# The thirteen looped rounds of a layer written out one behind the other in a six-layer transformer kernel

## The reference

```python
for i in range(DEPTH):                    # 6 layers
    x = attn_layer(shift_tokens(x), Wqkv[i], q_scale[i], k_scale[i], Wo[i]) + x
    x = ffn_layer(shift_tokens(x), ln_g[i], ln_b[i], W1[i], b1[i], W2[i], b2[i]) + x
```

## Time and profile before

| | us |
|---|---|
| median of three runs (lowest, highest) | 3637.79 (3636.72, 3644.33) |
| the profiled execution | 3636.09 |
| its span from first to last instruction | 3634.3 |
| PE busy in the span | 3397.6 (93%) |
| DVE busy | 3109.7 |
| ACT busy | 2520.1 |
| POOL busy | 1849.6 |

### The profile page before, as it was taken

The page is one execution under the profiler, slowest core; times in us unless marked ns, Lnnn a source line. Parts: engine busy times, 40 slices in busy tenths (PEclk is TensorE's granted clock), DMA queues, the critical chain, the costliest instruction groups (busy, mean ns, idle before and its releaser), DMA issues.

```text
span 3634.3 us, 161649 instructions
## 1 busy us (share of the span) xinstructions
PE 3397.6 (93%) x63524; PEld 2729.1 (75%) x63524; DVE 3109.7 (86%) x6016; ACT 2520.1 (69%) x4543; POOL 1849.6 (51%) x1604
## 2 busy tenths in 40 slices
PE   5857999999999999999999999999999999999997
PEld 2325888878788877788887788887788887788885
DVE  8987888888788888788888788888788888888884
ACT  2015777777777777777777677777677777777774
POOL 1434655554555555456555465555455564555561
PEclk9988999999999999999999999999999999999998
DMA  2002423323333323333233432332423332323333
GB/s 83 12 26 54 103 60 79 75 57 82 87 77 77 71 62 77 89 79 74 57 79 70 96 75 60 76 78 56 107 63 73 79 73 61 77 66 70 79 75 79
DMA packets 186363, 261.00 MB, mean 72 GB/s; under 512 B 31670, under 2 KB 89908, under 8 KB 185396
## 3 DMA queue, kind: packets, MB, share of 16 engines
q1 hardware_dynamic: 186164, 258.24, 31.6%
HBM read 22.30 MB, written 4.19 MB: 7 GB/s over the span
## 4 chain that ended last, share of the span: by engine, by line
PE 83%; issue 8%; DVE 5%; ACT 1%; POOL 1%; SPq 1%; DMA 0%; DVEq 0%; ACTq 0%; POOLq 0%
PE bank L667 10%; PE bank L654 9%; PE bank L719 9%; PE obank L701 8%; PE bank L752 7%; PE bank L630 7%; PE bank L632 5%; PE bank L631 5%; PE bank L677 5%; PE bank L711 4%; PE bank L645 3%; PE bank L759 3%; PE bank L647 2%; PE bank L646 2%; PE bank L739 1%
## 5 line engine op out<-in xcount | busy, mean ns | idle before, releaser
L977 POOL TENSOR_TENSOR qn<-qn,rinv 128x512 f32<-128x512 f32 x768 | 799.0, 1056 | 1305.0 <-DVE rinv L1224 1305.0
L971 POOL TENSOR_TENSOR qn<-ropec,ropes 128x512 f32<-128x512 f32 x768 | 991.3, 1302 | 257.6 <-DVE ropes L1176 216.1
L852 ACT ACTIVATE sq<-bank 128x512 f32<-128x512 f32 x768 | 458.3, 598 | 195.9 <-PE bank L632 169.3
L1184 DVE TENSOR_REDUCE ss<-sq 128x8 f32<-128x512 f32 x768 | 496.4, 676 | 84.8 <-ACT sq L852 84.8
L1175 DVE TENSOR_TENSOR ropec<-bank,rots 128x512 f32<-128x512 f32 x768 | 525.0, 684 | 18.5 <-ACT sq L852 12.1
L1176 DVE TENSOR_TENSOR ropes<-bank,rots 128x512 f32<-128x512 f32 x768 | 521.6, 679 | 0.0
L654 PE MATMUL bank<-ident,qn 128*128 128x128 f32 x3072 | 470.9, 276 | 26.1 <-ACT qT L870 18.8
L654 PEld LDWEIGHTS bank<-ident,qn 128*128 128x128 f32 x3072 | 369.3, 142 | 94.9 <-POOL qn L977 26.1
L667 PEld LDWEIGHTS bank<-kT,qT 64*32 64x32 f32 x24576 | 362.9, 107 | 96.5 <-issue 96.1
L667 PE MATMUL bank<-kT,qT 64*32 64x64 f32 x24576 | 422.2, 217 | 12.6 <-issue 6.7
L630 PE MATMUL bank<-wqkv_hi,xs_hi 128*128 128x512 f32 x768 | 365.5, 476 | 66.8 <-issue 42.7
(11 more groups left out here) (138 smaller groups left out, 6239.6 us busy)
## 6 DMA issues: line engine op xcount, KB each, us to landing
V<-Vt SPq DMA_DIRECT2D x576, 260.0 KB, 4.4
V<-Vt SPq DMA_DIRECT2D x192, 130.0 KB, 4.5
V<-Vt SPq DMA_DIRECT2D x192, 65.0 KB, 4.1
xres<-X SPq DMA_DIRECT2D x96, 128.0 KB, 2.1
X<-x SPq DMA_DIRECT2D x96, 128.0 KB, 2.0
wqkv_raw<-L_ffn_Wqkv SPq DMA_DIRECT2D x6, 1536.0 KB
xraw<-X SPq DMA_DIRECT2D x97, 64.0 KB, 2.0
xraw<-X SPq DMA_DIRECT2D x97, 63.8 KB, 1.9
```

The costliest lines, as they stand in the source:

```text
L971: pool.tensor_tensor(qn[:, c, :], ropec[:, c % ROPE_RING, :], ropes[:, c % ROPE_RING, :], ALU.add).then_inc(rope_sum.sem, 1)
L977: pool.tensor_tensor(heads8(qn[:, c, :]), heads8(qn[:, c, :]), rinv[:, 8 * c:8 * c + 8].unsqueeze(2).broadcast_to([P, 8, DH]), ALU.mult).t ...
L1184: dve.tensor_reduce(ss[:, 8 * c:8 * c + 8], heads8(sq[:, c % 2, :]), AX.X, ALU.add).then_inc(ss_done.sem, 1)
```

## The change

The two loops over rounds 3 to 15 become Python loops, so that the thirteen rounds are written into each engine's program one behind the other. The loop over the layers (L304) stays a hardware loop. The steps, their order within an engine and all tiles are as before.

```diff
@@ def pipeline(eng, body, conv_a=None, loads=None):
             with eng.Fori(0, DEPTH - 1) as l:
                 loads and loads(l + 1)
-                with eng.Fori(3, NB) as g:
+                for g in range(3, NB):
                     body(l * NB + g + 1, g, (0, 1, 2, 3), None, {2: l, 3: l})
                 conv_a and conv_a(l + 1)
...
             last = (DEPTH - 1) * NB
-            with eng.Fori(3, NB) as g:
+            for g in range(3, NB):
                 body(last + g + 1, g, (0, 1, 2, 3), None, {2: DEPTH - 1, 3: DEPTH - 1})
```

## The result

The changed kernel takes 3649.43 us in the median of 13 runs (3643.89 to 3662.32), the kernel before 3638.73 in 13 runs on the same chips (3632.57 to 3644.33). The ratio is 1.0032, 95% interval [1.0022, 1.0043]. The prediction was 3616 us, and 3603 to 3641 as its range, so it is wrong in sign and the result lies outside.

The account below looks back on a forecast made before the run. The prediction took PE, busy for 93% of the span, to bound the kernel, so its idle time counts. Terms -27.4 + 3 - 4 - 1.7 + 3.8 + 5 = -21.3 us gave 3616 us, range 3603 to 3641.

Parts of the forecast that it names:

- Term 1, the branches back: At PE's turns between looped rounds, 72 branches back go, 0.39 us each (0.33 in layer 5): -27.4 us.
- Term 2, the old edges: PE's existing instruction-block edges: round 0's stops go, -4; layer 5's round 3, -1.7; its rounds 4, 8, 12, +1.5, +1.4, +0.9.
- Term 2, the new edges: PE's block edges in newly written-out rounds: 0.1 us for some 30 blocks, +3; rounds 5, 8, 11, 14 no stop.
- Term 3, SP at the layer loop: At the layer loop's branch, SP's longer code may need fetching, 2.5 to 4 us late: +5 us (0 to +12).
- Costed at nothing: Fresh code on DVE, ACT and POOL, 100 instructions or fewer in 33 us, and PE's fetch traffic: no cost.
- Rival 2: Fresh code starves PE in the dense stretch, some 1.6 us a round, time near 3725 us; chance 0.14.
- Rival 1: The turns' idle time comes back elsewhere in the rounds, time near 3640 us, no change; chance 0.14.
- Rival 3: Instruction fetches hide entirely, SP's too, as the Trainium skill has it, time 3605 us; chance 0.08.

Follow-up runs that it names:

- PE only: Only PE's thirteen rounds written out, against the kernel before; SP, DVE, ACT and POOL keep their loops: 3626.37 us.
- SP only, weights later: Against the kernel before, SP alone written out and the next layer's weight transfers issued in rounds 4 to 7: 3627.14 us, ratio 0.9967.
- all but SP: PE, DVE, ACT and POOL written out, SP keeps its loops, against the kernel before: 3629.59 us.
- SP only: Only SP written out, against the kernel before, weight transfers left at the head of round 3: 3657.34 us.
- the weights later: PE alone written out, SP writing out rounds 3 to 7 and issuing the next layer's weights in rounds 4 to 7, against the kernel before: 3644.08 us.
- PE only, 16 places: PE alone written out, with 16 semaphore increments at the head of its program moving its edges, against the kernel before: 3613.97 us, ratio 0.9939.

## Why the prediction was wrong, step by step

**Term 1, the branches back: right.** 0.79 us from start to start, rounds 5, 6, 9 and 12 at 32.94 to 33.02 us in layers 0 to 4. All 72 turns give the -27.4 of the sum.

**Term 2, the old edges: right but for one.** Round 0 lost 4.0 us (-4 predicted). Layer 5's round 3 lost 1.9; the stop and its turn were put at 2.0. Layer 5's rounds 4 and 8 have stops of 1.60 and 1.2 us as foretold, 1.3 and 1.1 us over their turns' gain; round 12, put at 0.9, has none. Queue 8 has 521 packets (515).

**Term 2, the new edges: here it failed.** The step is "rounds 5, 8, 11, 14 those of round 1: no stop", with "0.1 for some 30 such blocks, +3". The DMA view of layer 2's round 1, from 22 to 25 us into it, has no instruction packet at all in the changed kernel (only data on q1), and from 25 to 28 us it has this one:

```profile
q8 instruction: 1, 0.02, 3.1%
```

The same stretch of 22 to 25 us with PE only written out, the same code on PE:

```profile
q1 hardware_dynamic: 249, 0.21, 23.8%
q8 instruction: 1, 0.02, 2.9%
```

In the trace the packet begins 26.28 us into the round in the first and 23.79 in the second. PE's own steps stand within 0.1 us of each other in the two (the last L701 ahead of it starts 25.62 and 25.54 us into the round), so PE does not come to the block later. The packet does not queue behind others either: in rounds 1 of layers 1 to 5 of the changed kernel no packet of any queue begins in the 2 us ahead of it (the DMA share of 0.00 from 1424.00 to 1426.50 above), and with PE and DVE written out it is the same. The round's own edges had moved (193 to 240 in my count, by the change itself), which I had in no sum. Round 1 costs +13.2. Round 11 shows the same with the same code in each layer: the packet begins 23.5 us into the round in layers 1 and 3 (no stop), at 25.6 to 25.7 in layers 0, 2 and 4 (stops of 1.53, 1.51, 1.24), and these three rounds are together 7.3 us over the turns' gain. The other new edges of rounds 4 to 14 come to 8.4 (18.1 in all, less 7.3 for round 11 and 2.4 for layer 5), where I had 3 for all of them, round 1 at nothing. Written-out rounds 1 and 2 of before had no such stops, and that was no proof: it was one draw of places.

**The term that was missing, the clock behind a stop.** I priced a stop at its idle time. The rounds above are 1.4 to 1.5 us busier as well, so a stop of 1.5 to 1.9 us can cost nearly double. It does not always: round 1 of layer 2 with PE and DVE written out has a stop as long, and the clock stays at 1.00 and PE's busy time at 32.90:

```profile
1427.22 0.44 PE L667 MATMUL bank<-kT,qT 64*32 64x64 f32 x17 [1.90 <-issue]
```

```profile
1398.33:1433.36 35.03, 32.90 (x660) 27.44 (x657) 28.91 (x59) 26.04 (x48) 19.79 (x19) 1.00 0.32 71
```

**Term 3, SP at the layer loop: the engine was right, the path and the size were not.** I had SP 2.5 to 4 us later, through the next x, at +5 (0 to +12). SP is later by 4.1 us. Layer 2 in the changed kernel, between the last of V's transfers and the first weights, has 1495.62 - (1487.38 + 3.28) = 4.96 us:

```profile
1487.38 3.28 SPq L470 DMA_DIRECT2D V<-Vt  x4
1495.62 0.35 SPq L418 DMA_DIRECT2D wqkv_raw<-L_ffn_Wqkv  x1
```

and before it had 1489.40 - (1485.95 + 2.54) = 0.91:

```profile
1485.95 2.54 SPq L470 DMA_DIRECT2D V<-Vt  x3
1489.40 0.34 SPq L418 DMA_DIRECT2D wqkv_raw<-L_ffn_Wqkv  x1
```

ACT then waits for x in round 4 of layer 1 for 1.42 us (0.88 before), but PE starts that round without idle time, so x is not the path.

It is the weights. They now run while PE fetches for its densest stretch, and PE stops there once, for 2.81 us (layer 2; 2.24 to 2.84 in layers 1 to 4, where before the longest stop in the same step was 1.18 to 1.53):

```profile
1505.95 0.32 PE L701 MATMUL obank<-V,PT 64*32 64x65 f32 x9 [2.81 <-issue]
```

Round 3 of layers 0 to 4 is 9.0 us longer in sum in spite of its five turns, so 11 us. With the weights elsewhere the late branch costs nothing that the intervals show (SP only, weights later); with SP looped, round 3 is 15.4 us shorter than in the change (all but SP). The prediction itself had the parts: that the weights' traffic makes the fetch queue in round 3, and that SP would be late with them. It did not put the two together. That the late weights delay the block, and not something else that comes with them, is argued from the place of the stop; what the runs show is that the late branch costs only where the weights follow it. How much of the cost in "SP only" is the stop and how much the wait for `qn` behind it, I did not separate.

**"Costed at nothing": wrong for DVE.** PE and DVE written out have round 1's stops, PE only has not. DVE does not run short itself: in round 1 of layer 2 none of its waits is "issue". With its code written out PE's packet begins later (26.15 us into the round for 23.79), and how the one brings the other is open.

**Rivals.** Rival 2 (fresh code starves PE) was nearest: not in each round, as it had it, but in round 1, round 3 and some of rounds 11. Rival 1 has no part, as the turns' gain is there in each clean round. Rival 3 fails by the stops of 1.2 to 2.8 us in the changed kernel. The rule of the Trainium skill behind it ("Runtime: NRT & Kernel Launch", section "Instruction fetch mechanics") is that crossing a block is mostly hidden. The trace agrees by number, with 17 stops of over 0.4 us inside the rounds for 521 blocks, but those 17 are 28 us in sum, as much as the turns bring. The same section gives the fetch that a taken branch can force as one reason why kernels prefer full unrolling. Here a branch whose body stays costs 0.39 us, and a late block a stop of 1.2 to 3.3 (the longest with the weights later).

**The sum.** -27.4 for the turns, -4.0 round 0, -3.4 round 2, +13.2 round 1, +9.4 round 3 over its turns, +18.1 rounds 4 to 14 over theirs, +0.8 round 15 and tail, +1.0 for the start: +7.7 us, the difference of the spans. Against the forecast of -21.3 that is 29.0 us more: 26 are the new edges (13.2, 7.3 and 8.4 for 3), 6 round 3 of layers 0 to 4 (11 for 5). Round 2's part is open: it is -0.3 with PE only, -2.1 with PE only and 16 places, -3.3 with all but SP.

## What to carry to other kernels

Before a hardware loop is unrolled, ask engine by engine: a branch whose body stays in the engine is a small, fixed price, and to write it out pays on the engine that bounds (PE alone: -12 us), not on one that then misses at an outer loop and issues transfers late (SP alone: +18 us). Where PE runs fresh code, look for stops inside a step at edges of 256 instructions, and before giving the change up, move the edges with a few instructions where PE is idle anyway: here 16 of them were worth 26 us, and 32 of them 1 us, since they brought stops elsewhere. So the places have to be counted or tried. Big transfers don't belong where PE fetches code for a dense stretch. The best version measured writes out all engines but SP and moves PE's edges by 16 places: 3612.50 us, 0.9927 of before; PE alone with the same 16 is at 0.9939, and the intervals overlap.

## What the runs showed of the hardware that was not expected

- The packet of a block of PE's code begins at different times for the same code and the same place (round 11: 23.5 or 25.6 to 25.7 us into the round), with no other packet in its way. What chooses is open. DVE's written-out code is enough to make the late one the rule in round 1 at the change's edges (stops in all of layers 1 to 5), and is not needed for it elsewhere (PE only, 16 places: two of these five). With the edges 32 places earlier the early time came in all five, DVE's code written out.
- With big transfers on the queues a block's packet begins later and PE stops for it: at the end of round 4 of layer 2, with `Wqkv` moving, 3.3 us later than with PE only, a stop of 3.22 us.
- A stop of 1.9 us is followed by PE at 1.2 GHz in one execution (L677's products 1.06 us for 0.60, granted clock 0.52) and not in another of nearly the same program; stops of 1.53 and 1.51 us in round 11 of layers 0 and 2 likewise (busy 32.90 and 34.45 us). The runs don't show what decides.
- SP's branch back over the layer's turn took 0.3 us to its next instruction at 123 instructions, and 4.2 to 4.6 us at 317.
